# A new order for VectorE, ScalarE and TensorE in the attention stage of a gated cross-attention block with routed experts

## The chip, the cores and the metric

The kernel runs on one core of a Trainium2 chip. The time is the device time of one execution in microseconds (us). The five engines of the core work through their own lists of instructions, each strictly in order, and meet only at semaphores: TensorE (PE: matmuls, transposes), VectorE (DVE), ScalarE (ACT), GpSimd (POOL) and SyncE (SP, which here only starts transfers).

## The reference

Eight sequences of 112 tokens with 512 channels, and for each a context of 375 tokens. The block computes:

```python
x = x + tanh(g_xattn) * xattn(layernorm(x), ctx)
x = x + tanh(g_ffn)   * experts(layernorm(x))

def xattn(h, cond):                      # 16 query heads in 8 groups, head size 128
    ln_out = ln(h)
    q, k, v, qx = fp8_linear(ln_out, ...)     # inputs rounded to fp8, times weights
    kx, vx = split(cond @ w_kv_x)
    q, k, qx, kx = ln(q), ln(k), ln(qx), ln(kx)   # per head, over 128 values
    core = softmax(q k^T / sqrt(d)) v         # 112 x 112 per head
    xout = softmax(qx kx^T / sqrt(d)) vx      # 112 x 375 per head
    return fp8(concat(core, xout) / smooth) @ wproj * scale

def experts(x):                          # 8 experts, the best 2 per token
    return sum_i w_i * (silu(x @ Wg[i]) * (x @ Wu[i])) @ Wd[i]
```

## The kernel before

There are four stages: quantising the inputs (to about 60 us), attention (to about 845 us), the output projection (to about 980 us), and the experts. The change is in attention alone.

Attention runs over four groups of heads (four query heads each, `g`), and within a group over the eight sequences. A position `(g, u)` is one step. Queries and keys are made in tiles of 128 rows (seven tiles for 896 tokens), so that the positions u = 0 to 6 have a tile and u = 7 has none. The work is a pipeline of two: step `s` projects position s, while the position before, `t`, goes through softmax and the product with the values. I call the attention part of one t a unit; it is counted from the first score matmul of t to the first of the next.

In an ordinary step PE does: project 0 (queries), transposes of the normed queries of t (turn 0, 1), project 1 (cross queries), turn 2 (keys) and turn 3 (cross keys), project 2, the self scores (`p_self`) and two of four cross scores (`p_cross`), turn 4, project 3, the transposes of the softmax results (turn_self, turn_cross 0), cross score 2, turn_cross 1, cross score 3, project 4, outputs 0 (`p_out`), turn_cross 2 and 3, project 5, outputs 1.

The parts of a step on the other engines:
- ACT: `take` j (L689) empties the PSUM bank of projection j and writes the squares of its values; `turned` n (L713) writes a transposed piece with weight and bias; `exp_self` (L734) and `exp_cross` h (L743); `c_high` (L666), the high part of a context chunk. take 3, 4 and 5 wait until turn 4 of the unit before has read `nkx`.
- POOL: `c_low` k (L615), the low part `c_lo` of a context chunk, 128x500, and `rstd` j (L598), which makes `rs`, the reciprocal root of the variance, for the rows of projection j. It goes through them as c_low 0, rstd 0, c_low 1, rstd 1, c_low 2, rstd 2, rstd 3, rstd 4, rstd 5.
- DVE: `sums` j (L1025) adds up the squares, `scale` j (L1034) multiplies `nq` (j = 0), `nqx` (1), `nk` (2) or a part of `nkx` (3 to 5) by `rs`; `max_self` (L1042), `max_cross` h (L1056), `norm_self` (L1048), `norm_cross` h (L1062); `take_self` (L1069) and `take_cross` h (L1074) copy transposed results out of PSUM (`pselfT`, `pcrossT`); `inputs` (L1016) fills `xqs` for the next step; `smoothed` (L1080) empties `p_out`; `exponents` and `rounded` (L1087, L1098) round the result to fp8 and write `cat`.

The order on each engine is written out by hand in functions `step` and, for positions without a tile, `last_step` (ACT L771, L750; PE L953, L929; DVE L1139, L1106). The steps are named: "first" is the very first, "queries" is u = 6 and "keys" u = 7 of the groups 0 to 2, in which weights of the next group are split as well, "new" is u = 0 of groups 1 to 3. In group 3 and in the very last step, which projects nothing (A is false), there is no weight work. Each engine waits only at its own next instruction: one that isn't ready holds back all behind it.

Of the kernel before, what the change touches and what calls it, by code (L numbers as in the profile page):

```python
# [396 lines left out]
def before(pos):  # L397
    g, u = pos
    return (g, u - 1) if u > 0 else (g - 1, B - 1)
# [42 lines left out]
def attention(nc, c, sb, ps, sem, ctxT, wproj, catd, vec, ident, mhalf, epst, xq, smi,  # L442
# [207 lines left out]
    def _(act):  # L650
# [99 lines left out]
        def last_step(s, t, g, change):  # L750

            turned(t, 0)
            turned(t, 1)
            take(s, 2)
            turned(t, 2)
            c_high(s, 1)
            if change == "keys": w_high(g, 2, change)
            turned(t, 3)
            exp_self(t)
            exp_cross(t, 0)  # L760
            exp_cross(t, 1)
            turned(t, 4)
            take(s, 3)
            c_high(s, 2)
            if change == "keys": w_high(g, 3, change)
            take(s, 4)
            exp_cross(t, 2)
            exp_cross(t, 3)
            take(s, 5)
# [43 lines left out]
    def _(pe):  # L813
# [139 lines left out]
        def step(s, t, g, change, k):  # L953
            A, Q = s is not None, t is not None
# [10 lines left out]
            if not A: score_self(t)  # L965
            if Q: turn(t, 3)
            if A: project(s, 2, g)
            if A and Q: score_self(t)
# [19 lines left out]
    def _(v):  # L988
# [13 lines left out]
        def w_low(g, n):  # L1002

            v.wait_ge(wh_done[n], g + 1)
            split_low(v, n).then_inc(wl_done[n], 1)
# [100 lines left out]
        def last_step(s, t, g, change):  # L1106
# [5 lines left out]
            if change == "keys": rounded(before(t))  # L1112
# [10 lines left out]
            norm_cross(t, 3)  # L1123
            take_cross(t, 2)
            take_cross(t, 3)
            smoothed(t, 0)
            if change == "keys": inputs((s[0] + 1, 0))
            scale(s, 4)
            if change == "keys": w_low_half(g, 1, 1)
            smoothed(t, 1)  # L1130
            scale(s, 5)
            if change == "keys":
                w_low(g, 2)
                w_low(g, 3)
            else:
                exponents(t)
                rounded(t)

        def step(s, t, g, change, k):  # L1139
# [5 lines left out]
            if change == "new": w_low(g, 4)  # L1145
            if Q: max_self(t)
            if Q: max_cross(t, 0)
            if Q: max_cross(t, 1)
            if change == "new": exponents(before(t))
            if Q: norm_self(t)  # L1150
            if Q: norm_cross(t, 0)
            if Q: norm_cross(t, 1)
            if Q: take_self(t)
            if A: sums(s, 1)
            if Q: take_cross(t, 0)
            if Q: max_cross(t, 2)
            if A: scale(s, 0)
            if Q: take_cross(t, 1)
            if Q: max_cross(t, 3)
            if A: sums(s, 2)  # L1160
            if Q: norm_cross(t, 2)
            if Q: norm_cross(t, 3)
            if A: scale(s, 1)
            if A: scale(s, 2)
            if A: inputs((s[0], s[1] + 1))
            if change == "new": rounded(before(t))
# [10 lines left out]
            if Q and change != "queries": rounded(t)  # L1177
# [729 lines left out]
```

## Time and profile before

Three runs took 1220.67, 1217.78 and 1221.2 us, median 1220.67.

| | |
|---|---|
| the profiled execution's own time | 1220.67 us |
| its span, first to last instruction | 1218.2 us |
| busy: PE, DVE, ACT, POOL | 1096.6, 805.3, 726.3, 495.4 us |
| 32 units of attention | from 90.5 to about 843 us |
| PE clock granted, attention stage | 1.0 of full speed from 81 to 845 us |
| DVE `nq` scale, 28 in all | mean 718 ns |
| DVE `ysum` and `cat` (rounded), 32 each | mean 623 and 625 ns |

A busy time is a mean over stages with different limits. PE is busy 99% of most of the attention stage. There the timeline of one unit tells more: an engine's row gives the start, the duration, and in brackets how long the engine had been idle and whose work ended the wait. Instructions of one engine overlap at their ends, so that the distance of two starts is often somewhat shorter than the first one's duration.

### The profile page before, as it was taken

The numbers are of one execution on the slowest core, as the hardware profiler recorded it, in microseconds if no ns is written. First come the engines' busy times: TensorE is split into PE (matmuls) and PEld (weight loads), VectorE is DVE, ScalarE is ACT, GpSimd is POOL, SyncE is SP. The second block draws the span as 40 slices with busy tenths as digits, with TensorE's granted clock in tenths as the row PEclk, the third lists the DMA queues.
The fourth block names the chain that finished last, engine by engine and source line by source line (L and its number), as shares of the span: only waits on it lengthen the run. The fifth ranks groups of instructions, "written<-read, shape, count | busy, mean of one in ns | idle before, by whom it ended". The sixth has DMA issues, their size and how long they took to land. (4 is left out here: it accounts for less than half of the span.)

```text
span 1218.2 us, 19518 instructions
## 1 busy us (share of the span) xinstructions
PE 1096.6 (90%) x5656; PEld 895.5 (74%) x5656; DVE 805.3 (66%) x1611; ACT 726.3 (60%) x2082; POOL 495.4 (41%) x584
## 2 busy tenths in 40 slices
PE   1089999999999999999999999995999839999996
PEld 1068888778888877888877888874888727777885
DVE  7967877897788787777788777676334675564100
ACT  7967878855888865688875655762121514343432
POOL 3064544444545435444535454440000314565432
PEclk9589999999999999999999999998999759999999
DMA  5042111105111115111112311101546255865220
GB/s 199 0 175 65 43 34 41 52 15 198 50 42 43 34 34 200 39 41 51 42 34 80 107 42 34 49 26 46 178 147 233 90 203 177 246 182 163 48 44 0
DMA packets 51713, 107.38 MB, mean 88 GB/s; under 512 B 5984, under 2 KB 26464, under 8 KB 49568
## 3 DMA queue, kind: packets, MB, share of 16 engines
q1 hardware_dynamic: 46912, 97.00, 24.3%
q0 software_dynamic: 4704, 9.18, 3.3%
q8 instruction: 49, 0.80, 0.3%
q14 instruction: 48, 0.39, 0.1%
HBM read 91.48 MB, written 16.52 MB: 89 GB/s over the span
## 5 line engine op out<-in xcount | busy, mean ns | idle before, releaser
L618 POOL TENSOR_TENSOR c_lo<-c_raw,c_hi 128x500 fp32r<-128x500 f32 x96 | 123.9, 1291 | 208.9 <-ACT c_hi L669 208.9
L612 POOL TENSOR_TENSOR rs<-va,mhalf 125x2 f32<-125x2 f32 (+1 forms) x180 | 199.3, 1107 | 14.3
L827 PE MATMUL p_proj<-w_hi,xqs 128*128 128x512 f32 (+2 forms) x464 | 157.4, 359 | 42.3 <-DVE w_lo L540 41.0
L854 PE MATMUL p_proj<-w_hi,c_hi 128*125 128x512 f32 x384 | 164.5, 429 | 1.3 <-POOL c_lo L618 1.3
L854 PE MATMUL p_proj<-w_hi,c_lo 128*125 128x512 f32 x384 | 151.4, 394 | 0.0
L854 PE MATMUL p_proj<-w_lo,c_hi 128*125 128x512 f32 x384 | 151.4, 394 | 0.0
L827 PE MATMUL p_proj<-w_lo,xqs 128*128 128x512 f32 (+2 forms) x464 | 148.2, 340 | 0.0
L827 PEld LDWEIGHTS p_proj<-w_hi,xqs 128*128 128x128 f32 (+1 forms) x464 | 86.7, 187 | 51.0 <-issue 43.0
L605 POOL TENSOR_TENSOR va<-ss,epst 125x2 f32<-125x2 f32 (+1 forms) x180 | 45.9, 255 | 167.6 <-DVE ss L1030 99.0
L747 ACT ACTIVATE pcross<-p_cross,nmax 112x375 f32<-112x375 f32 x128 | 73.6, 584 | 51.3 <-DVE nmax L1059 51.2
L897 PE MATMUL p_cross<-kxT,qxT 128*112 128x375 f32 x256 | 97.7, 484 | 0.8 <-ACT kxT L723 0.8
L1321 PE MATMUL p_acc<-p_hi,p_catr 128*128 128x512 f32 x224 | 89.0, 397 | 9.1 <-DVE p_lo L1366 9.1
L827 PEld LDWEIGHTS p_proj<-w_lo,xqs 128*128 128x128 f32 (+1 forms) x464 | 86.9, 187 | 8.2
L1321 PE MATMUL p_acc<-p_lo,p_catr 128*128 128x512 f32 x224 | 88.7, 396 | 0.0
L854 PEld LDWEIGHTS p_proj<-w_hi,c_hi 128*125 128x125 f32 x384 | 71.4, 186 | 21.2 <-issue 3.3
L854 PEld LDWEIGHTS p_proj<-w_hi,c_lo 128*125 128x125 f32 x384 | 71.2, 186 | 17.8
L854 PEld LDWEIGHTS p_proj<-w_lo,c_hi 128*125 128x125 f32 x384 | 71.4, 186 | 17.1
L924 PE MATMUL p_out<-pcrossT,valx 125*128 125x224 f32 x384 | 83.7, 354 | 0.0
L1291 ACT ACTIVATE p_hi<-shared 128x512 fp32r<-128x512 f32 x32 | 20.2, 634 | 90.3 <-PE p_acc L1321 80.0
L924 PEld LDWEIGHTS p_out<-pcrossT,valx 125*128 125x128 f32 x384 | 73.2, 191 | 0.3
L1082 DVE TENSOR_TENSOR yb<-p_out,smg 128x448 bf16<-128x448 f32 x64 | 39.7, 621 | 50.9 <-PE p_out L924 50.9
L709 ACT ACTIVATE nkx<-p_proj 125x256 f32<-125x256 f32 x96 | 38.4, 400 | 58.2 <-PE p_proj L854 58.2
(240 smaller groups left out, 2852.5 us busy)
## 6 DMA issues: line engine op xcount, KB each, us to landing
c_raw<-in_ctxT SPq DMA_DIRECT2D x96, 250.0 KB, 2.6
shared<-in_w_in SPq DMA_DIRECT2D x16, 1024.0 KB, 9.0
shared<-in_wproj SPq DMA_DIRECT2D x32, 256.0 KB, 2.9
raw_g<-in_Wg SPq DMA_DIRECT2D x8, 1024.0 KB, 6.6
raw_u<-in_Wu SPq DMA_DIRECT2D x8, 1024.0 KB, 6.9
raw_d<-in_Wd SPq DMA_DIRECT2D x8, 1024.0 KB, 5.7
cat_scratch<-cat SPq DMA_DIRECT2D x32, 224.0 KB, 2.0
shared<-cat_scratch SPq DMA_DIRECT2D x2, 1792.0 KB, 8.2
```

The lines of the kernel that those rows point to most:

```text
L605: pool.tensor_tensor(va[0:rows, lo:hi], ss[0:rows, lo:hi], epst[0:rows, lo:hi], ALU.add).then_inc(va_done, 1)
L612: pool.tensor_tensor(rs[0:rows, lo:hi], va[0:rows, lo:hi], mhalf[0:rows, lo:hi], ALU.pow).then_inc(rs_done, 1)
L618: pool.tensor_tensor(flat(c_lo[:, k, :, :]), flat(c_raw[:, k, :, :]), flat(c_hi[:, k, :, :]).bitcast(F32), ALU.subtract).then_inc(cl_done, 1)
L709: act.activation(nkx[0:CT, j - 3, :], bank[0:CT, 0:256], ACT.Copy)
L747: act.activation(pcross[0:T, h, :], p_cross[0:T, h % 2, 0:TC], ACT.Exp, bias=nmax[0:T, 4 + h:5 + h], accum_out=lsum[0:T, 4 + h:5 + h]).the ...
L827: m = pe.matmul(out, xqs[:, n, k, 0:rows], (w_hi, w_lo)[i % 2][:, k, lo:lo + w], start=(i == 0), stop=(i == 2 * KB - 1))
L854: m = pe.matmul(bank[0:CT, :], a[:, ch, k, :], w[:, k, CKX:CV], start=(i == 0), stop=(i == 3 * KB - 1))
L897: pe.matmul(p_cross[0:T, h % 2, 0:TC], qxT[:, t[1] % 2, h, :], kxT[:, h // HPG, :], start=True, stop=True).then_inc(sx_rdy, 1)
L924: m = pe.matmul(p_out[:, HPG * T:2 * HPG * T], valx[0:CT, par, k, g * P:(g + 1) * P], flat(pcrossT[0:CT, k, HPG * g:HPG * (g + 1), :]), st ...
L1082: v.tensor_tensor(yb[:, g * 4 * T:(g + 1) * 4 * T].rearrange("p (a t) -> p a t", t=T), p_out[:, 0:4 * T].rearrange("p (a t) -> p a t", t=T ...
L1291: act.activation(w_hi[:, n % 2, :], w_raw[:, n % 4, :], ACT.Copy).then_inc(hi_done, 1)
L1321: m = pe.matmul(acc[:, j, :], catr[:, n % 2, j * P:(j + 1) * P], w[:, n % 2, :], start=(first and part == 0), stop=(last and part == 1), s ...
```

## The change

Three engines get another order in attention; no instruction's work is altered. On ACT, take 3 moves ahead of exp_self in the steps without a tile. On PE the self scores move behind turn 3 in the very last step. On DVE, `sums` 1 moves ahead of `max_self` and `scale` 0 ahead of `max_cross` 0 in all steps that project a tile, and `sums` 2, `scale` 1 and `scale` 2 each move up a place; `exponents` and `rounded` of the unit before move up in a "new" step; `rounded` moves from the "keys" step into the end of the "queries" step; and in steps without a tile `inputs`, `scale` 4 and one piece of `w_low` move up.

```diff
@@ ACT, last_step
             turned(t, 3)
+            take(s, 3)
             exp_self(t)
             exp_cross(t, 0)
             exp_cross(t, 1)
             turned(t, 4)
-            take(s, 3)
             c_high(s, 2)
@@ PE, step
             if Qt: turn(t, 2)
-            if not A: score_self(t)
             if Q: turn(t, 3)
             if A: project(s, 2, g)
-            if A and Q: score_self(t)
+            if Q: score_self(t)
@@ DVE, last_step
             max_cross(t, 1)
-            if change == "keys": rounded(before(t))
             norm_self(t)
...
             norm_cross(t, 3)
+            if change == "keys": inputs((s[0] + 1, 0))
+            scale(s, 4)
             take_cross(t, 2)
             take_cross(t, 3)
             smoothed(t, 0)
-            if change == "keys": inputs((s[0] + 1, 0))
-            scale(s, 4)
             if change == "keys": w_low_half(g, 1, 1)
+            if change == "keys": w_low(g, 2)
             smoothed(t, 1)
             scale(s, 5)
             if change == "keys":
-                w_low(g, 2)
                 w_low(g, 3)
@@ DVE, step
             if change == "new": w_low(g, 4)
+            if A: sums(s, 1)
+            if change == "new": exponents(before(t))
             if Q: max_self(t)
+            if A: scale(s, 0)
             if Q: max_cross(t, 0)
             if Q: max_cross(t, 1)
-            if change == "new": exponents(before(t))
             if Q: norm_self(t)
             if Q: norm_cross(t, 0)
             if Q: norm_cross(t, 1)
+            if change == "new": rounded(before(t))
             if Q: take_self(t)
-            if A: sums(s, 1)
+            if A: sums(s, 2)
             if Q: take_cross(t, 0)
             if Q: max_cross(t, 2)
-            if A: scale(s, 0)
+            if A: scale(s, 1)
             if Q: take_cross(t, 1)
             if Q: max_cross(t, 3)
-            if A: sums(s, 2)
+            if A: scale(s, 2)
             if Q: norm_cross(t, 2)
             if Q: norm_cross(t, 3)
-            if A: scale(s, 1)
-            if A: scale(s, 2)
             if A: inputs((s[0], s[1] + 1))
-            if change == "new": rounded(before(t))
...
-            if Q and change != "queries": rounded(t)
+            if Q: rounded(t)
```

In an ordinary step, DVE's list before, from the first sums to the second. `ss<-sq` is sums, `nmax` the maxima, `linv` the reciprocals, `pselfT` take_self; the scale of `nq` comes three rows further down:

```order
L1030 TENSOR_REDUCE ss<-sq 128x4
L1045 TENSOR_REDUCE nmax<-p_self 112x4
L1059 TENSOR_REDUCE nmax<-p_cross 112x1 x2
L1051 RECIPROCAL linv<-lsum 112x4
L1053 TENSOR_TENSOR pself<-pself,linv 112x448
L1064 RECIPROCAL linv<-lsum 112x1
L1066 TENSOR_SCALAR pcross<-pcross,linv 112x375
L1064 RECIPROCAL linv<-lsum 112x1
L1066 TENSOR_SCALAR pcross<-pcross,linv 112x375
L1072 COPY pselfT<-p_tr 112x448
L1030 TENSOR_REDUCE ss<-sq 128x4
```

The same place after (line numbers are one less):

```order
L1029 TENSOR_REDUCE ss<-sq 128x4 x2
L1044 TENSOR_REDUCE nmax<-p_self 112x4
L1038 TENSOR_TENSOR nq<-nq,rs 128x512
L1058 TENSOR_REDUCE nmax<-p_cross 112x1 x2
L1050 RECIPROCAL linv<-lsum 112x4
L1052 TENSOR_TENSOR pself<-pself,linv 112x448
L1063 RECIPROCAL linv<-lsum 112x1
L1065 TENSOR_SCALAR pcross<-pcross,linv 112x375
L1063 RECIPROCAL linv<-lsum 112x1
L1065 TENSOR_SCALAR pcross<-pcross,linv 112x375
L1071 COPY pselfT<-p_tr 112x448
L1029 TENSOR_REDUCE ss<-sq 128x2
```

The second sums and the scale of `nq` have moved from behind take_self to the two sides of max_self.

ACT in a "keys" step, before (-) and after (+). `kxT` is turned 3 and then turned 4, `nkx`, `valx` and `sqx` are take 3, `pself` and `pcross` the exponentials:

```order
 L723 ACTIVATE kxT<-p_cross,vec 128x375
-L739 ACTIVATE pself,lsum<-p_self,nmax 112x112 x4
-L747 ACTIVATE pcross,lsum<-p_cross,nmax 112x375 x2
-L723 ACTIVATE kxT<-p_tr,vec 128x375
-L709 ACTIVATE nkx<-p_proj 125x256
-L710 ACTIVATE valx<-p_proj 125x256
-L685 ACTIVATE sqx,ss<-p_proj 125x128 x2
+L709 ACTIVATE nkx<-p_proj 125x256
+L710 ACTIVATE valx<-p_proj 125x256
+L685 ACTIVATE sqx,ss<-p_proj 125x128 x2
+L739 ACTIVATE pself,lsum<-p_self,nmax 112x112 x4
+L747 ACTIVATE pcross,lsum<-p_cross,nmax 112x375 x2
```

The four reads of take 3 have moved ahead of the four exponentials of the self scores, the two of the cross scores and turned 4.

## Rows read from the trace of the kernel before

**Rows 1.** List of waits, PE: engine, line, released by: us in total, times, longest.
```profile
PE p_out L921 <- DVE pcrossT L1077: 8.6, 24, 1.4
```
**Rows 2.** Timeline, PE, an ordinary unit: start us, us, engine, line, instruction [idle before].
```profile
331.27 0.94 PE L890 MATMUL p_self<-kT,qT 128*112 128x112 f32 x8
...
336.43 0.55 PE L904 MATMUL p_tr<-ident,pself 112*112 112x112 f32 x4
...
337.79 0.55 PE L911 MATMUL p_tr<-ident,pcross 112*125 112x112 f32 x3
...
346.05 0.39 PE L854 MATMUL p_proj<-w_lo,c_hi 128*125 128x512 f32 x1
346.27 0.39 PE L854 MATMUL p_proj<-w_hi,c_lo 128*125 128x512 f32 x1
346.87 0.65 PE L921 MATMUL p_out<-pselfT,val 112*128 112x224 f32 x2 [0.21 <-DVE pcrossT L1077]
...
355.54 0.94 PE L890 MATMUL p_self<-kT,qT 128*112 128x112 f32 x8
```
**Rows 3.** Timeline, DVE, the same unit.
```profile
332.25 0.62 DVE L1045 TENSOR_REDUCE nmax<-p_self 112x4 f32<-112x448 f32 x1 [1.58 <-PE p_self L890]
...
334.39 0.18 DVE L1051 RECIPROCAL linv<-lsum 112x4 f32<-112x4 f32 x1 [0.33 <-ACT pself L739]
334.60 0.63 DVE L1053 TENSOR_TENSOR pself<-pself,linv 112x448 f32<-112x448 f32 x1
...
335.86 0.42 DVE L1066 TENSOR_SCALAR pcross<-pcross,linv 112x375 f32<-112x375 f32 x1
337.02 0.62 DVE L1072 COPY pselfT<-p_tr 112x448 f32<-112x448 f32 x1 [0.74 <-PE p_tr L904]
337.56 0.67 DVE L1030 TENSOR_REDUCE ss<-sq 128x4 f32<-128x512 f32 x1
...
339.02 0.68 DVE L1039 TENSOR_TENSOR nq<-nq,rs 128x512 f32<-128x512 f32 x1
```
**Rows 4.** Timeline, ACT, the same unit.
```profile
331.71 0.66 ACT L677 ACTIVATE sq<-p_proj 128x512 f32<-128x512 f32 x1
...
332.91 0.35 ACT L739 ACTIVATE pself<-p_self,nmax 112x112 f32<-112x112 f32 x1
...
334.24 0.58 ACT L747 ACTIVATE pcross<-p_cross,nmax 112x375 f32<-112x375 f32 x1
...
335.33 0.69 ACT L723 ACTIVATE kxT<-p_tr,vec 128x375 f32<-128x375 f32 x1
```
**Rows 5.** Timeline, POOL, the same unit.
```profile
332.41 1.01 POOL L612 TENSOR_TENSOR rs<-va,mhalf 128x4 f32<-128x4 f32 x1
...
333.39 1.26 POOL L618 TENSOR_TENSOR c_lo<-c_raw,c_hi 128x500 fp32r<-128x500 f32 x1
```
**Rows 6.** Timeline, POOL and DVE, the first step of attention.
```profile
75.84 1.27 POOL L618 TENSOR_TENSOR c_lo<-c_raw,c_hi 128x500 fp32r<-128x500 f32 x1
75.91 1.74 DVE L1039 TENSOR_TENSOR nq<-nq,rs 128x512 f32<-128x512 f32 x1 [1.29 <-POOL rs L612]
```
**Rows 7.** Timeline, several engines, a "keys" unit (from 426.1) and a "new" unit (448.5).
```profile
428.34 0.48 PE L881 MATMUL p_tr<-ident,nkx 125*128 125x125 f32 x3
...
431.32 0.41 ACT L709 ACTIVATE nkx<-p_proj 125x256 f32<-125x256 f32 x1
...
432.35 0.68 ACT L669 ACTIVATE c_hi<-c_raw 128x500 fp32r<-128x500 f32 x1
...
428.23 0.99 DVE L1059 TENSOR_REDUCE nmax<-p_cross 112x1 f32<-112x375 f32 x2
...
454.33 0.59 PE L904 MATMUL p_tr<-ident,pself 112*112 112x112 f32 x4 [0.52 <-DVE pself L1053]
...
464.24 0.62 DVE L1104 TENSOR_TENSOR cat<-ysum,ye 128x896 bf16<-128x896 bf16 x1
...
466.28 0.65 PE L921 MATMUL p_out<-pselfT,val 112*128 112x224 f32 x2 [1.40 <-DVE pcrossT L1077]
```

## The prediction

> **What bounds the kernel now.** I read the list of waits first, then the timeline of one ordinary unit of the attention stage engine by engine, then the two odd units at a change of head group. All edits lie in the attention stage; what follows it starts when it ends, so a microsecond lost or won there is one in the total. In the list of waits the largest term of TensorE (PE) that belongs to the units is one on VectorE (DVE): 24 waits for `pcrossT`, 8.6 us in all [rows 1]. So PE works nearly without a stop and the stage can't gain much: its waits are a few tenths of a microsecond in each of 32 units.
>
> An ordinary unit lasts 24.27 us: from the score matmuls `p_self` at 331.27 to the next ones at 355.54 [rows 2]. I count from 331.27; "at 5.16" means 5.16 us after it. PE's only real wait stands near the unit's end: the last projection matmul starts at 346.27 and `p_out` at 346.87 [rows 2]. That is 0.60 us, where the start before is only 0.22 us away (346.05, and 0.23 to 0.24 elsewhere), so the wait is about 0.36 us. It is for the last copy into `pcrossT` (take_cross 3). The list's 24 cases are 20 ordinary units (five per group) and four others. The gain to be had in ordinary units is at most 20 x 0.36 = 7.2 us.
>
> How much room DVE's other results have is read from the same timeline. The softmax chain is: max_self (ends at 1.60), exp_self on ACT (starts at 1.64), the two max_cross, the reciprocal (at 3.12), norm_self (at 3.33 to 3.96), the second norm_cross (starts at 4.59, ends at 5.01), then take_self at 5.75, right after PE's transposes at 5.16 [rows 2 to 4]. PE's second transpose of `pcross` (turn_cross 1) starts at 6.52, 0.15 us after take_self ends at 6.37: it reuses the PSUM bank that take_self empties. So norm_self has some 1.2 us of room, but the chain norm to take_self to turn_cross 1 has only what take_self waits for: 0.74 us idle before it [rows 3].
>
> **The change in an ordinary unit.** DVE now does sums 1 before max_self, and scale 0 (the tensor_tensor on `nq`) between max_self and max_cross 0. Both stood behind take_self before.
> - sums 1 waits for ACT's squares, which end at 0.44 + 0.66 = 1.10 [rows 4]. It starts at 1.14 and holds DVE 0.59 us, the distance from it to the next instruction after 337.56 [rows 3] (0.67 us by itself, less the overlap of its end). max_self starts at 1.73 instead of 0.98, ends at 2.35, and exp_self starts at 2.39: ACT's exp chain is 0.75 us later.
> - scale 0 needs `rs`, which POOL finishes at 2.15, and POOL then starts the second c_lo at 2.12 without a gap; it runs 1.26 us, to 3.38 [rows 5]. Here is the point on which the sum rests. Both instructions read two SBUF tensors. In the first step of the stage the same pair met: c_lo started at 75.84 and took 1.27 us, the scale of `nq` started 0.07 us behind it and took 1.74 us [rows 6], where it takes 0.68 us elsewhere [rows 3]. It ended 0.54 us after c_lo. So scale 0, which can only start at 2.26 behind max_self, ends at 3.38 + 0.54 = 3.92, not at 2.94.
> - max_cross 0 and 1 follow at 3.84 to 4.83 (0.99 us for both where PE's scores are there, as at 428.23 [rows 7]), the reciprocal at 4.74, norm_self at 4.95. Between norm_self and take_self the order and the durations stay: the second norm_cross starts 1.26 us after norm_self, ends at 6.63, and take_self runs from 6.55 to 7.17. PE's turn_cross 1 starts 0.15 us later, at 7.32 instead of 6.52: **0.80 us lost**. The other two paths agree or are shorter: norm_self ends at 5.58 and PE's transposes of `pself` go from 5.16 to 5.64, 0.48 late; exp_cross 0 starts at 4.42 instead of 2.97 (max_cross 0 is now last), so turned 4 ends 1.46 later, at 6.21 instead of 4.75 (4.06 and 0.69 long [rows 4]), and turn_cross 0 goes to about 6.27, 0.72 late.
> - Behind that, DVE is shorter by what was moved ahead: sums and scale of `nqx` are moved up, and the wait for the third `rs` mostly goes. I find take_cross 3 ending at about 14.6, while PE, 0.80 late, wants it at 15.24 + 0.80 = 16.0. So the wait of **0.36 us goes**.
>
> The unit becomes 24.27 + 0.80 - 0.36 = 24.71 us. Twenty units: +8.8 us. The last unit with a full tile in each group (four) has no such wait to give back: 4 x 0.80 = +3.2 us.
>
> The Trainium skill, page "SBUF — State Buffer", section "Who interferes with whom", says that a DVE instruction with two SBUF inputs contends with a GpSimd one that reads SBUF, that the first to issue has the shared port pair for its whole length, and that the other blocks fully. The trace's 1.74 us is that, with 0.54 us left after c_lo instead of the full 0.68. By the rule to the letter scale 0 would end 0.14 us later and 24 units would cost 3.4 us more, 1241 in all. I go by the row.
>
> **The unit before and after a change of group (three times).** On ACT take 3 now stands ahead of exp_self. It must wait for PE's transposes turn 4, which read the `nkx` it overwrites: they start at 428.34 and end at 428.82, and exp_self could start at 428.34 before. take 3 is four reads of PSUM, from 431.32 to 432.35, 1.03 us [rows 7]. exp_self so starts at about 429.9 instead of 428.34. DVE there was late for its reciprocal anyway, because of `rounded`, which has gone to the unit before. I get PE about 0.7 us late at that unit's end. In the next unit ("new") DVE does sums 1, three exponents and scale 0 ahead of norm_self, with the exponents now even ahead of max_self, and `rounded`, two instructions of 0.62 us [rows 7], between norm_cross 1 and take_self, on the path that PE waits for. PE waited there already (454.33, the wait before it 0.52 by the row, 0.68 by starts) and again for take_cross 3, 1.40 us by the row [rows 7]. The work that was moved ahead is taken from behind, so the second wait goes while the first grows to about 3.5 us. Net for both units together I take +1.2 us; the bounds are -1.5 (both waits of the row go) and +3. Three times: +3.6 us.
>
> **The last group and the last step.** Here the same move on ACT has less cover: exp_self goes from 1.65 after its `p_self` to about 3.8, 2.2 us later, of which the room of 0.74 and the earlier transposes take a part: +1.2 us. score_self behind turn 3 in the last step is one swap of two short PE groups: +0.1 us.
>
> **Edits at nothing.** inputs and scale 4 ahead of take_cross 2 in the "keys" step: PE there waits for smoothed 0 and its own transposes, and inputs fills this; it is in the 0.7 above. `w_low` of piece 2 before smoothed 1: hidden behind PE's outputs 1. POOL's and SyncE's own orders don't change; c_lo 2 comes later by ACT's delay, and PE needs it only at 12.4 (project 5), so it is covered.
>
> **Sum.** 8.8 + 3.2 + 3.6 + 1.3 = 16.9 us. The profiled execution took 1220.67 us (span 1218.2), which is also the median of the three runs, so 1237.6 us.
>
> **Rivals.** A change of 0.3% (3.7 us) is about what a measurement here can tell from none.
> - *Faster: scale 0 and c_lo don't hold each other.* If scale 0 ended by 2.94, the max_cross would end at 3.85, norm_self would start at 4.08 and end at 4.70, and PE's transposes at 5.16 would find it ready; take_self would come at 5.75 as now. Then 20 x 0.36 = 7.2 us are won, the group changes are about even without the stalls, and 1.3 us is lost in the last group: 1214.8 us. It decides at scale 0's end: up to some 3.1 the chain has room. For it speaks that rows 6 are one of only two such meetings of this form; against it that both were equal, and that POOL's c_lo has no idle before it [rows 5], so DVE can't come first. 8 in 100.
> - *Smaller loss: the delays overlap with waits that I count as room used up.* With half the 0.80, ordinary units are even, the others cost 4 x 0.4, and with 3.6 and 1.3 the sum is +6.5: 1227 us. 10 in 100.
> - *No change:* that, and the group changes gain instead of losing (by 1.5 each, the bound above): 1221. 4 in 100.
> - *Larger loss: the wait for take_cross 3 stays.* scale 2 now stands ahead of the last two norm_cross, and scale 1 can meet the third c_lo; if these give DVE back its delay, 7.2 us are not won: 1244.8 us. 13 in 100.
>
> The forecast itself, 1231 to 1243, has 65 in 100. The chance of slower is 0.65 + 0.10 + 0.13 = 0.88, of the same 0.04, of faster 0.08. The range for 8 in 10 goes from 1226 to 1246: it takes in the small loss and the large one and leaves out the faster case.
>
> **What would show it.** In the trace after: ordinary units 24.7 us apart; 24 scales of `nq` between max_self and max_cross, about 1.65 us long instead of 0.68; a wait of PE before the transposes of `pself` and of `pcross` in every unit with a full tile, and the 24 waits for `pcrossT` before `p_out` gone; in the "new" units a PE wait of over 2 us before take_self's copy is done. PE's granted clock through the attention stage should stay at its upper level, 2.4 GHz (the page's clock line shows no fall there through PE waits of 1.4 us [rows 7]). Wrong at the root would be scales of `nq` of 0.7 us in that place. Wrong in size would be a unit that is late by the full 1.5 us of max_cross, or one with the wait at `p_out` still there.

## The result and the profile after

The changed kernel takes 1236.85 us (median of 4 runs, 1235.88 to 1242.38), the kernel before 1220.93 us beside it (4 runs, 1217.78 to 1222.62). The ratio is 1.0158, 95% interval 1.0138 to 1.0179: 15.9 us slower, where the prediction said 16.9. The profiled execution of after took 1238.48 us with a span of 1236.6 us, 18.4 us more than before. Over all 21 executions of after on record (1235.88 to 1242.56) the median is 1240.6 us, 19.7 us over before; where the text below compares with 1236.85 or with 15.9, it takes the median of the four.

The list of waits of after, PE (us in total, times, longest):

```profile
PE p_tr L904 <- DVE pself L1052: 17.2, 32, 2.2
PE p_out L921 <- DVE yb L1081: 3.8, 4, 1.0
PE p_tr L911 <- ACT kxT L723: 2.3, 8, 0.3
PE p_tr L911 <- DVE pselfT L1071: 1.5, 2, 0.8
```

The 24 waits for `pcrossT` [rows 1] are gone, and PE now waits for norm_self in all 32 units (before in 4). The scales of `nq` in after (ns shortest/median/longest, first and last start):

```profile
L1038 DVE TENSOR_TENSOR nq<-nq,rs x28: 675/1658/1732, 75.9 to 810.0; 128x512 f32<-128x512 f32 x28
```

An ordinary unit after, from 339.71 (answering to the unit from 331.27 before). DVE [rows 3]:

```profile
340.86 0.69 DVE L1029 TENSOR_REDUCE ss<-sq 128x4 f32<-128x512 f32 x1 [1.74 <-ACT sq L677]
341.46 0.61 DVE L1044 TENSOR_REDUCE nmax<-p_self 112x4 f32<-112x448 f32 x1
341.99 1.65 DVE L1038 TENSOR_TENSOR nq<-nq,rs 128x512 f32<-128x512 f32 x1
343.56 0.99 DVE L1058 TENSOR_REDUCE nmax<-p_cross 112x1 f32<-112x375 f32 x2
...
344.68 0.62 DVE L1052 TENSOR_TENSOR pself<-pself,linv 112x448 f32<-112x448 f32 x1
...
346.26 0.61 DVE L1071 COPY pselfT<-p_tr 112x448 f32<-112x448 f32 x1
...
347.99 1.13 DVE L1038 TENSOR_TENSOR nqx<-nqx,rs 128x512 f32<-128x512 f32 x1
```

POOL [rows 5]:

```profile
340.86 1.01 POOL L612 TENSOR_TENSOR rs<-va,mhalf 128x4 f32<-128x4 f32 x1
341.84 1.25 POOL L618 TENSOR_TENSOR c_lo<-c_raw,c_hi 128x500 fp32r<-128x500 f32 x1
```

PE [rows 2]:

```profile
339.71 0.95 PE L890 MATMUL p_self<-kT,qT 128*112 128x112 f32 x8
...
345.36 0.60 PE L904 MATMUL p_tr<-ident,pself 112*112 112x112 f32 x4 [0.32 <-DVE pself L1052]
...
347.08 0.50 PE L911 MATMUL p_tr<-ident,pcross 112*125 112x112 f32 x3
...
355.75 0.54 PE L921 MATMUL p_out<-pselfT,val 112*128 112x224 f32 x2
...
364.31 0.94 PE L890 MATMUL p_self<-kT,qT 128*112 128x112 f32 x8
```

The scale of `nq` starts 0.15 us behind c_lo, takes 1.65 us instead of 0.68 and ends at 343.64, 0.55 us after c_lo (343.09). The maxima, norm_self, norm_cross and take_self follow it without a wait. Of the 28 scales of `nq` 24 take 1.65 to 1.67 us, the one of the first step 1.73 us as before, and the three of the "new" steps 0.68 us. The scale of `nqx` meets the third c_lo and takes 1.13 us instead of 0.68 in the same 24 units. PE's second transposes of `pcross` start 7.37 us into the unit instead of 6.52, and `p_out` no longer waits. The unit lasts 24.60 us.

Where the 18.4 us of span are, by the starts of the first `p_self` of each unit (us, before and after):

| | units | before, each | after, each | difference in all |
|---|---|---|---|---|
| ordinary | 20 | 24.28 | 24.60 | +6.6 |
| started in the "queries" step | 4 | 22.02 | 22.80 | +3.1 |
| "keys" | 3 | 22.40 | 23.18 | +2.3 |
| "new" | 3 | 26.46 | 29.77, 27.77, 28.41 | +6.6 |
| last group's unit without a tile | 1 | 15.82 | 18.61 | +2.8 |
| last unit, to the projection's first `p_acc` | 1 | 23.59 | 20.69 | -2.9 |
| before the first unit | | 90.46 | 91.75 | +1.3 |
| behind attention | | 368.2 | 366.8 | -1.4 |

No edit acts in the stretches of the last two rows. Over the 13 profiled kernels of this case these stretches take 90.5 to 91.9 and 366.8 to 369.7 us, so the total of one profile says no more than within some 3 us. The two rows above them belong together: in the last step `p_self`, with which a unit begins, now stands behind turn 3, and 1.6 us pass from the last unit to the one without a tile by the counting alone.

The "new" units are the surprise. The second of them after, PE:

```profile
466.31 0.59 PE L904 MATMUL p_tr<-ident,pself 112*112 112x112 f32 x4 [1.51 <-DVE pself L1052]
467.19 0.75 PE L911 MATMUL p_tr<-ident,pcross 112*125 112x112 f32 x3 [0.29 <-ACT kxT L723]
467.73 1.46 PE L897 MATMUL p_cross<-kxT,qxT 128*112 128x375 f32 x2
```

POOL and DVE in the same unit:

```profile
457.24 1.26 POOL L618 TENSOR_TENSOR c_lo<-c_raw,c_hi 128x500 fp32r<-128x500 f32 x1 [6.02 <-ACT c_hi L669]
457.30 3.36 DVE L540 TENSOR_TENSOR w_lo<-shared,w_hi 128x2048 fp32r<-128x2048 f32 x1
...
462.01 1.35 DVE L1095 TENSOR_SCALAR ye<-ye 128x896 bf16<-128x896 bf16 x1
463.28 0.61 DVE L1044 TENSOR_REDUCE nmax<-p_self 112x4 f32<-112x448 f32 x1
...
465.62 0.63 DVE L1052 TENSOR_TENSOR pself<-pself,linv 112x448 f32<-112x448 f32 x1
...
467.87 0.62 DVE L1103 TENSOR_TENSOR cat<-ysum,ye 128x896 bf16<-128x896 bf16 x1
468.41 0.62 DVE L1071 COPY pselfT<-p_tr 112x448 f32<-112x448 f32 x1
```

Windows of after, PE (stretch, its length, PE busy and instructions, granted clock, DMA share, GB/s), in the first, second and third "new" unit and behind the second:

```profile
270.00:278.00 8.00, 7.53 (x23) 0.61 0.39 126
466.00:471.00 5.00, 4.41 (x15) 0.66 0.34 88
471.00:476.00 5.00, 5.00 (x28) 1.00 0.33 115
664.00:669.00 5.00, 4.20 (x14) 0.66 0.57 187
```

PE waits 1.51 us for norm_self, where it waited 0.52 [rows 7], then 0.29 us, and in the first and the third of these units another 0.68 and 0.80 us ahead of turn_cross 1. Right behind the waits its clock is at the lower level, 1.2 GHz, for a part of the windows: two cross scores take 1.46 us there, where the same two take 0.80 at the upper level. DVE starts max_self 3.81 us into the unit instead of 1.41, since sums 1, the exponents and a longer `w_lo` stand ahead of it. `w_lo` of this form takes 2.28 us where it meets no c_lo, 2.76 in this place before and 3.36 here. `ye` takes 1.35 us beside a c_lo; elsewhere it takes 0.39 or 0.40. Before, the granted clock was 1.0 from 81 to 835 us; the table ahead of the prediction says to 845, which is wrong:

```profile
835.10:838.40 3.30, 3.30 (x11) 0.50 0.00 0
```

That fall comes up again where the prediction is gone through.

### The profile page after: what moved, and what is told of

Read it like the earlier page. It is cut to its first block and busy times, and to the rows that moved or that the text cites. A ratio compares the mean times of both kernels' runs of the same rounds, so it can differ in the third digit from the quotient of the medians.

```text
span 1236.6 us, 19518 instructions
## 1 busy us (share of the span) xinstructions
PE 1104.4 (89%) x5656; PEld 898.8 (73%) x5656; DVE 817.1 (66%) x1611; ACT 726.4 (59%) x2082; POOL 471.6 (38%) x584
## 5 line engine op out<-in xcount | busy, mean ns | idle before, releaser
L618 POOL TENSOR_TENSOR c_lo<-c_raw,c_hi 128x500 fp32r<-128x500 f32 x96 | 121.3, 1263 | 265.9 <-ACT c_hi L669 264.6
L612 POOL TENSOR_TENSOR rs<-va,mhalf 125x2 f32<-125x2 f32 (+1 forms) x180 | 152.4, 847 | 14.2 <-POOL va L605 0.2
L605 POOL TENSOR_TENSOR va<-ss,epst 125x2 f32<-125x2 f32 (+1 forms) x180 | 68.8, 382 | 155.2 <-ACT sqx L685 155.1
L1029 DVE TENSOR_REDUCE ss<-sq 128x4 f32<-128x512 f32 (+1 forms) x84 | 49.6, 592 | 64.9 <-ACT sq L677 64.9
L854 PEld LDWEIGHTS p_proj<-w_hi,c_hi 128*125 128x125 f32 x384 | 72.5, 189 | 19.7 <-issue 2.3
L911 PEld LDWEIGHTS p_tr<-ident,pcross 112*125 112x125 f32 x384 | 53.5, 191 | 26.5 <-issue 13.7
```

The source lines that it names most:

```text
L605: pool.tensor_tensor(va[0:rows, lo:hi], ss[0:rows, lo:hi], epst[0:rows, lo:hi], ALU.add).then_inc(va_done, 1)
L612: pool.tensor_tensor(rs[0:rows, lo:hi], va[0:rows, lo:hi], mhalf[0:rows, lo:hi], ALU.pow).then_inc(rs_done, 1)
L618: pool.tensor_tensor(flat(c_lo[:, k, :, :]), flat(c_raw[:, k, :, :]), flat(c_hi[:, k, :, :]).bitcast(F32), ALU.subtract).then_inc(cl_done, 1)
L854: m = pe.matmul(bank[0:CT, :], a[:, ch, k, :], w[:, k, CKX:CV], start=(i == 0), stop=(i == 3 * KB - 1))
L911: m = pe.transpose(p_tr[0:CT, 1 - h % 2, k * T:(k + 1) * T], pcross[0:T, h, k * CT:(k + 1) * CT], ident[0:T, 0:T])
L1029: v.tensor_reduce(ss[0:rows, lo:hi], sq[0:rows, j % 2, 0:(hi - lo) * HD].rearrange("p (h d) -> p h d", d=HD), AX, ALU.add).then_inc(rd_don ...
```

## The experiments

All on one core, each timed against the kernel before on the same chip. "Unit" is as above. The medians are of 4 to 10 executions (after: the four). The unit columns are from one profiled execution (us, each; * marks a unit in a part of which the granted clock was at the lower level):

| run | median us | ratio to before, 95% | ordinary | queries | keys | "new" |
|---|---|---|---|---|---|---|
| before | 1220.9 | | 24.28 | 22.02 | 22.40 | 26.47, 26.46, 26.46 |
| after | 1236.9 | 1.0138 to 1.0179 | 24.60 | 22.80 | 23.18 | 29.77*, 27.77*, 28.41* |
| a | 1221.1 | 0.9990 to 1.0036 | 23.91 | 22.10 | 23.18 | 26.97, 28.47*, 26.97 |
| b | 1217.0 | 0.9955 to 0.9984 | 23.91 | 22.08 | 23.19 | 27.71*, 26.04, 26.09 |
| c | 1217.5 | 0.9960 to 0.9987 | 24.28 | 22.03 | 22.41 | 25.53, 25.52, 25.51 |
| d | 1233.3 | 1.0079 to 1.0116 | 24.63 | 22.80 | 22.41 | 27.79*, 26.95, 26.96 |
| e | 1233.8 | 1.0082 to 1.0126 | 24.62 | 22.80 | 23.17 | 27.58*, 25.92, 25.94 |
| f | 1240.7 | 1.0145 to 1.0196 | 24.63 | 22.80 | 23.91 | 26.97, 27.99*, 28.03* |
| g | 1207.1 | 0.9862 to 0.9909 | 23.84 | 22.04 | 22.42 | 25.33, 25.32, 25.33 |
| h | 1213.5 | 0.9924 to 0.9966 | 23.83 | 22.03 | 23.89, 23.89, 25.02* | 25.09, 25.09, 25.09 |
| i | 1241.6 | 1.0135 to 1.0178 | 24.61 | 22.81 | 23.17 | 27.79*, 29.92*, 27.87* |
| j | 1235.2 | 1.0100 to 1.0137 | 24.62 | 22.80 | 22.60 | 28.45*, 26.97, 28.53* |
| k | 1206.3 | 0.9856 to 0.9890 | 23.82 | 22.01 | 22.40 | 25.27, 25.27, 25.29 |

**a. Scale 0 back behind take_self, all else changed.**

```diff
             if Q: max_self(t)
-            if A: scale(s, 0)
             if Q: max_cross(t, 0)
@@
             if Q: take_self(t)
+            if A: scale(s, 0)
             if A: sums(s, 2)
```

> The changed kernel with one edit undone in part: scale 0 (nq) stands behind take_self again, sums 1 stays ahead of max_self. Theory 1 (scale 0 meets POOL's second c_lo and is held by it, 1.65 us instead of 0.68 ahead of the max_cross): without the meeting the ordinary unit goes from 24.60 us to about 23.95, the queries unit loses its 0.8, so about 1221 us. Theory 2 (the later exponentials, because sums 1 stands ahead of max_self, are the cost): nearly nothing changes, 1234 to 1237 us.

1221.08 us. Moving this one instruction brings the ordinary unit from 24.60 to 23.91 and takes back 15.8 of the 15.9 us (19.5 of the 19.7 by all executions of after). The scales of `nq` have a median of 681 ns again. sums 1 still stands ahead of max_self here, so sums 1 ahead costs at most the 0.07 us by which the unit is over g's below.

**b. The changed kernel, the second c_lo on 4 of its 500 columns** in all steps with a tile but the first (that low part of the context is left out).

```diff
+            n = 4 if k == 1 and has_tile(s) and s is not FIRST else KB * CT
-            pool.tensor_tensor(flat(c_lo[:, k, :, :]), flat(c_raw[:, k, :, :]), ...
+            pool.tensor_tensor(flat(c_lo[:, k, :, :])[:, 0:n], flat(c_raw[:, k, :, :])[:, 0:n], ...
```

> The changed kernel, order untouched, but POOL's second c_lo of each step with a tile works on 4 columns instead of 500 (the low part of that chunk is left out, so its results are less exact). Theory 1: scale 0 takes 0.68 us, ordinary unit about 23.9 us, total about 1219.5 us. Theory 2: still about 1237 us, since the order on VectorE is the same.

1217.0 us. DVE's list is that of the changed kernel, word for word, and the loss is gone. DVE in an ordinary unit of b:

```profile
333.12 0.61 DVE L1045 TENSOR_REDUCE nmax<-p_self 112x4 f32<-112x448 f32 x1
333.65 0.68 DVE L1039 TENSOR_TENSOR nq<-nq,rs 128x512 f32<-128x512 f32 x1
```

POOL beside it:

```profile
333.51 0.20 POOL L619 TENSOR_TENSOR c_lo<-c_raw,c_hi 128x4 fp32r<-128x4 f32 x1
```

Same place, same neighbours, a short c_lo: 0.68 us. So the cost is the meeting, not the place. The "new" unit is 0.9 us shorter as well (26.04 and 26.09), since `ye` meets nothing there.

**c. The same on the kernel before**, as the control (the same low part left out).

> The kernel before with the same short second c_lo (the same part left out), as the control for the other: both theories say no change, 1221 us within 2, unit 24.27 us, since nothing on VectorE meets that c_lo in the old order.

1217.5 us, 3.2 less than before and more than I expected. All of it is in the "new" units, 26.46 to 25.52 (2.8 us in three). In an ordinary unit of before the second c_lo meets the maxima and the start of norm_self and costs nothing (24.28 both). In the "new" unit it meets the exponents. DVE before, then c:

```profile
451.75 1.35 DVE L1093 TENSOR_SCALAR ye<-yb 128x896 uint16<-128x896 uint16 x1
```

```profile
451.62 0.40 DVE L1094 TENSOR_SCALAR ye<-yb 128x896 uint16<-128x896 uint16 x1
```

The kernel before had such collisions already, and I had not seen them. Besides these three, norm_cross 2 (`pcross`) takes 1.01 or 1.02 us instead of 0.42 in 27 units, each time beside the third c_lo. DVE and POOL in the ordinary unit of rows 2 and 3:

```profile
341.01 1.01 DVE L1066 TENSOR_SCALAR pcross<-pcross,linv 112x375 f32<-112x375 f32 x1
```

```profile
340.54 1.26 POOL L618 TENSOR_TENSOR c_lo<-c_raw,c_hi 128x500 fp32r<-128x500 f32 x1
```

c leaves these 27 as they are; what they cost comes up again under g. Against this control b is the same within the measurement: beside the collision all of the change comes to nothing (0.37 us won in each ordinary unit, and about as much lost at the changes of group and in the last group).

**d. The kernel before with scale 0 alone moved.**

```diff
             if Q: max_self(t)
+            if A: scale(s, 0)
             if Q: max_cross(t, 0)
@@
             if Q: max_cross(t, 2)
-            if A: scale(s, 0)
```

> The kernel before with one edit of the change alone: scale 0 between max_self and max_cross 0, sums 1 stays where it was. Theory 1: scale 0 waits for rs until 2.19 after p_self, meets c_lo and ends at the same 3.92, so the ordinary unit is 24.6 us as in the changed kernel, the queries unit 0.8 longer, total about 1230 us. Theory 2: exp_self keeps its time, so no loss, 1214 to 1221 us.

1233.34 us: one instruction makes 12.6 of the 15.9 us. DVE and, below, PE in an ordinary unit of d, whose `p_self` starts at 335.85:

```profile
336.83 0.62 DVE L1045 TENSOR_REDUCE nmax<-p_self 112x4 f32<-112x448 f32 x1 [1.58 <-PE p_self L890]
338.04 1.74 DVE L1039 TENSOR_TENSOR nq<-nq,rs 128x512 f32<-128x512 f32 x1 [0.59 <-POOL rs L612]
```

```profile
341.50 0.59 PE L904 MATMUL p_tr<-ident,pself 112*112 112x112 f32 x4 [0.33 <-DVE pself L1053]
```

max_self is on time here, 0.77 us earlier in the unit than in after, and it doesn't matter: scale 0 waits for `rs` and then ends 0.54 us after c_lo (337.98 + 1.26) all the same. c_lo's end sets the unit's chain, so the unit is 24.63 us with and without sums 1 ahead. My 0.59 us for sums 1 was right as a duration and is hidden under c_lo.

**e. The changed kernel, exponents and rounded of the "new" step back in their old places.**

```diff
-            if change == "new": exponents(before(t))
             if Q: max_self(t)
@@
             if Q: max_cross(t, 1)
+            if change == "new": exponents(before(t))
             if Q: norm_self(t)
@@
-            if change == "new": rounded(before(t))
             if Q: take_self(t)
@@
             if A: inputs((s[0], s[1] + 1))
+            if change == "new": rounded(before(t))
```

> The changed kernel with one part undone: in the three "new" steps DVE does the exponents behind max_cross 1 again (they stand ahead of max_self in the changed kernel) and rounded behind inputs again (it stands between norm_cross 1 and take_self). Everything else is as changed. Theory 1, that these moved instructions lie on PE's path to the transposes of pself and pcross and that the long wait there also costs PE its clock: the new unit, 29.8, 27.8 and 28.4 us in the changed kernel, comes down to about 27.3 (26.46 before, plus the 0.8 of scale 0), the stretches of some 3.4 us at the half clock at about 467 and 666 us go, and the keys unit stays at 23.2; total 1236.8 - 4 = about 1233. Theory 2, that the long new unit is the effect of scale 0 and sums 1 alone: the new units stay at 28 to 30 us and the total at 1237.

1233.84 us, as theory 1 said; the falls at 467 and 666 us are gone, one at 270 us stays. (This is 3.0 us under the median of four of after and 6.8 under that of all 21.) The "new" units without a clock fall are 25.93 us (I said 27.3). With the moves such a unit is 26.97 (a, f and j), so they cost 1.04 us a time. PE's waits show where: in f's first "new" unit, with the moves, three, and in e's second, with the moves undone, one.

```profile
268.20 0.59 PE L904 MATMUL p_tr<-ident,pself 112*112 112x112 f32 x4 [1.51 <-DVE pself L1052]
269.09 0.55 PE L911 MATMUL p_tr<-ident,pcross 112*125 112x112 f32 x3 [0.29 <-ACT kxT L723]
...
271.07 0.55 PE L911 MATMUL p_tr<-ident,pcross 112*125 112x112 f32 x3 [0.80 <-DVE pselfT L1071]
```

```profile
464.50 0.59 PE L904 MATMUL p_tr<-ident,pself 112*112 112x112 f32 x4 [1.66 <-DVE pself L1052]
```

The first wait doesn't depend on where the exponents stand (ahead of max_self or behind the maxima, DVE has done them before norm_self). By the waits, what costs is rounded between norm_cross 1 and take_self (0.80 us) and exp_self behind a late max_self (0.29). Neither of these two units had a clock fall; e had one in three "new" units, after three in three.

**f, i, j. The "keys" unit: ACT's take 3 back, DVE's rounded back, both back.**

```diff
@@ f and j: ACT, last_step
             turned(t, 3)
-            take(s, 3)
             exp_self(t)
@@
             turned(t, 4)
+            take(s, 3)
@@ i and j: DVE, last_step and step
             max_cross(t, 1)
+            if change == "keys": rounded(before(t))
             norm_self(t)
@@
-            if Q: rounded(t)
+            if Q and change != "queries": rounded(t)
```

> The changed kernel with ACT's one move undone: take 3 stands behind turned 4 again in the steps without a tile (three keys steps, and the one of the last group). Theory 1, that this move is the loss of 0.78 us in the keys unit: the keys unit goes from 23.18 back to about 22.4 us, three times, and the last group's from 18.61 to about 15.8; but its following unit, 21.25 now, goes up to about 24.2, since the two together lost nothing. Total 1236.8 - 2.3 = about 1234.5. Theory 2, that the keys unit's 0.78 comes from DVE's order (inputs and scale 4 ahead of take_cross 2): it stays at 23.2 and the total at 1237.

> The changed kernel with DVE's one move at the keys step undone: rounded stands between max_cross 1 and norm_self of the keys step again and not at the end of the queries step; ACT's take 3 stays ahead of exp_self. What is open is which edit costs the keys unit its 0.78 us (22.40 before, 23.18 after; with take 3 moved back it was 23.94, with a wait of 0.76 us for c_lo). Theory 1, that two edits each make exp_self late, rounded by making max_self 1.3 us late on DVE and take 3 by holding ACT, and that the later one decides: with only rounded put back take 3 still holds exp_self at 3.9 us, so the keys unit stays at 23.1 to 23.4 and the total at 1237. Theory 2, that rounded alone is the cause: keys unit 22.4, total 1234.5.

> The changed kernel with both undone, rounded back in the keys step and take 3 behind turned 4; inputs, scale 4 and w_low of piece 2 stay moved up in the steps without a tile. Theory 1, that both edits together are the loss and those that stay cost nothing there: the keys unit is 22.4 us as before, three times, the last group's unit near 15.8, total about 1234. Theory 2, that inputs and scale 4 ahead of take_cross 2 cost PE time too (its wait for yb at p_out was 0.81 us before and 0.99 after): keys unit 22.6 or more.

f failed its expectation: undoing take 3 made the unit longer, 23.91. In the queries step rounded now stands ahead of max_self, so max_self starts 2.94 us into the unit (1.62 before). exp_self is then late by itself, and with it turned 4, take 3 and c_high 2 behind it on ACT. PE, in f and then in j:

```profile
444.08 0.47 PE L854 MATMUL p_proj<-w_hi,c_hi 128*125 128x512 f32 x1 [0.76 <-POOL c_lo L618]
```

```profile
441.66 0.47 PE L854 MATMUL p_proj<-w_hi,c_hi 128*125 128x512 f32 x1 [0.44 <-POOL c_lo L618]
```

With rounded put back and take 3 ahead (i) the unit is 23.17, as in after: now ACT's four reads hold exp_self. With both back (j) it is 22.60. So either edit alone makes exp_self late: it starts 3.59 us into the unit in f, 3.89 in i and in after, 2.27 in j and before. With rounded moved, take 3 ahead even saves 0.73 us, since c_lo then comes in time. The last 0.20 us over before is what remains moved in j, `inputs` and scale 4 ahead of take_cross 2: PE's wait for `yb` at `p_out` is 0.98 us there and 0.81 before. The medians of f and i are 3.8 and 4.7 us over after's median of four, but 0.05 and 1.0 us over that of all 21, so neither differs from after by more than executions do among themselves.

**g. The kernel before, with two instructions in DVE's idle times:** sums 1 behind max_cross 1, scale 0 behind norm_cross 1.

```diff
             if Q: max_cross(t, 1)
+            if A: sums(s, 1)
@@
             if Q: norm_cross(t, 1)
+            if A: scale(s, 0)
             if Q: take_self(t)
-            if A: sums(s, 1)
@@
             if Q: max_cross(t, 2)
-            if A: scale(s, 0)
```

> The kernel before with only this: sums 1 directly behind max_cross 1 (the idle time of 0.33 us before the reciprocal), scale 0 directly behind norm_cross 1 (the idle 0.74 us before take_self), so that neither stands ahead of a maximum and scale 0 starts after the second c_lo has ended. Theory 1, that ordinary units can win only the wait for pcrossT at p_out and that this place costs nothing: scale of nq 0.68 us, ordinary units 23.8 to 23.95 us instead of 24.27, twenty times, new and keys units as before; total 1220.7 - 7 = about 1214. Theory 2, that anything ahead of take_self delays PE's transposes of pcross: units 24.2 to 24.4 us and 1221 or a little more.

1207.07 us, 1.15% faster than before. It reaches what the change was after, DVE's later work done earlier, without meeting c_lo: `nq` takes 682 ns (median), and there is no wait at `p_out`, PE in an ordinary unit of g, 10.32 us and 15.29 us into it:

```profile
337.71 0.54 PE L921 MATMUL p_out<-pselfT,val 112*128 112x224 f32 x2
...
342.68 0.54 PE L921 MATMUL p_out<-pselfT,val 112*128 112x224 f32 x2
```

The gain is 0.44 us in each of 20 ordinary units (8.7 us) and 1.14 in each "new" unit (3.4 us). I had expected 7 in all. The wait in rows 2 was read as 0.36 us and is worth 0.44; in the "new" units the wait of 1.40 us for take_cross 3 [rows 7] is gone, and one of 0.54 us ahead of turn_cross 1 has come. The order is not the whole reason. With sums 1 early POOL does the third c_lo 6.17 us into the unit instead of 9.27, it no longer meets norm_cross 2, and all 128 scalings of `pcross` take 0.41 or 0.42 us. Those 0.6 us a unit are more than the wait of 0.44, so the second collision alone could account for it; no run separates the two.

**h. g, with the exponents of the "new" step behind take_self and one `w_low` of the "keys" step behind max_cross 2**, into 1.72 us of DVE idle time.

```diff
-            if change == "new": exponents(before(t))
@@
             if Q: take_self(t)
+            if change == "new": exponents(before(t))
@@ last_step
             max_cross(t, 2)
+            if change == "keys": w_low(g, 2)
             scale(s, 3)
```

> The kernel of the run with sums 1 behind max_cross 1 and scale 0 behind norm_cross 1, and at the change of group: exponents of the new step behind take_self instead of behind max_cross 1, and w_low of piece 2 in the keys step behind max_cross 2 instead of behind smoothed 1. Theory 1, that PE's 0.5 and 1.4 us waits in the new unit are for DVE work that has room elsewhere: the new unit goes from 26.46 to about 25 us, three times; total about 1210. Theory 2, that the exponents only change places with another wait (for take_cross 3): the new unit stays within 0.5 us of 26.46 and the total is that of the other run, about 1214.

1213.47 us, slower than g by 6.4 us, which neither theory had. DVE, POOL and PE of h:

```profile
428.82 0.54 DVE L1059 TENSOR_REDUCE nmax<-p_cross 112x1 f32<-112x375 f32 x1
429.27 1.21 DVE L540 TENSOR_TENSOR w_lo<-shared,w_hi 128x1024 fp32r<-128x1024 f32 x1
```

```profile
428.86 2.73 POOL L618 TENSOR_TENSOR c_lo<-c_raw,c_hi 128x500 fp32r<-128x500 f32 x1 [6.71 <-ACT c_hi L669]
```

```profile
431.73 0.47 PE L854 MATMUL p_proj<-w_hi,c_hi 128*125 128x512 f32 x1 [1.91 <-POOL c_lo L618]
```

In DVE's idle time POOL was at work on c_lo: now DVE runs at its usual speed (1.21 us), c_lo takes 2.73 us instead of 1.25, and PE waits for it. In the third group the clock fell behind this wait as well (that "keys" unit is 25.02 us, the others 23.89).

**k. g with the exponents alone moved.**

> The kernel of the run with sums 1 behind max_cross 1 and scale 0 behind norm_cross 1 (1207.1 us) with only the exponents of the new step moved behind take_self; w_low of piece 2 in the keys step stays behind smoothed 1. In the run that had both of these moves the keys unit was 23.89 instead of 22.43, c_lo took 2.73 us beside w_low and PE waited 1.91 us for it, and the new unit was 25.09 instead of 25.33. Theory 1, that w_low beside c_lo is the whole loss of that run: keys unit 22.4, c_lo 1.25 us there, new unit 25.1, total 1207.1 - 0.7 = about 1206.4. Theory 2, that the loss came from elsewhere: keys unit over 23 and the total near 1213.

1206.27 us, ratio to before 0.9873 (0.9856 to 0.9890). c_lo is back at 1.25 us and the "keys" unit at 22.40: `w_low` beside c_lo was the loss of h. The exponents' place is worth 0.05 us a unit (25.28 for 25.33, I said 25.1), so k and g are equal within the measurement; the rest of h's shorter "new" unit, 25.09, came with `w_low`'s move. Both beat both kernels.

## Why the prediction was right, point by point

- **The collision, the root of it: right, and shown.** Said: scale 0 takes 1.65 us between max_self and max_cross and ends 0.54 us after c_lo. Measured: 1.65 us, 0.55 us after c_lo. b removes the collision and keeps the place, a removes the place; both remove the loss. The rival without a collision was put at 1214.8 us; b, less what c alone brings, makes it about 1220, no change: that rival's ordinary units were right (0.37 won), and its group changes weren't even.
- **Ordinary unit, said +0.80 - 0.36, measured +0.33.** The first term is 0.69 to 0.76: with scale 0 ahead the unit is 24.60 us, with it behind take_self 23.91 (a), in g 23.84. The chain came as said, PE's transposes of `pself` 5.65 us into the unit (said 5.64) and turn_cross 1 at 7.37 (said 7.32); a wait of its own before the transposes of `pcross`, also said, stands in no row of this unit. The second term was too small: the wait is worth 24.28 - 23.84 = 0.44 us and not 0.36. Together twenty units cost 6.6 us and not 8.8. The reading that this wait is take_cross 3's own place in DVE's list missed the stretched norm_cross 2 ahead of it (c).
- **Queries unit, said +0.80, measured +0.78.** Four times: 3.1 against 3.2.
- **The larger-loss rival, wait for take_cross 3 stays:** fallen, only one wait of 0.9 us is left of those in [rows 1]. Its mechanism does occur, `nqx` meets the third c_lo and takes 1.13 us, but this doesn't reach PE.
- **Change of group, said +3.6 us, measured +8.9.** This is the term that failed. "keys": I said 0.7 us late, it is 0.78, though by a cause that I had only half (rounded in the queries step makes max_self late too, 2.94 us into the unit instead of 1.62). "new": I netted a growing first wait against a vanishing second one and came to 0.5 us a time. Without a clock fall that is the measured number, 26.97 against 26.46, but by luck: a first wait grown from 0.5 to 3.5 us, less the 1.40, makes 1.6 us more than before, and I took 0.5. Measured are 1.51, 0.29 and 0.80 us, 2.6 in all, where before had 0.52 and 1.40; no single wait is over 2 us, as I had named for a sign. What I missed is the clock. I wrote that it should stay at its upper level, since PE's waits of 1.4 us had caused no fall before. The trace of before did show a fall inside attention, from 835.05 us, behind a wait of 2.23 us and one of 0.29 (its rows stand under the next point); I had read the clock line of the page alone. In after it fell in all three "new" units, for 0.8, 1.4 and 2.8 us (27.77, 28.41 and 29.77 less 26.97), 5.0 us in all. Before, PE's waits there were 0.52 and 1.40 us and 12 us apart; in after they are 1.51, 0.29 and up to 0.8 us within 3 us. What in these waits brings a fall no run isolates.
- **Last group, said +1.3, measured -0.1: both terms as said but for 0.1, hidden by a clock fall.** The unit without a tile is 2.79 us longer and the last unit 2.90 shorter. Of both, 1.6 us is the counting (`p_self` behind turn 3): with take 3 back the unit without a tile is 17.43 (f) or 17.42 (j), against 15.82. Take 3 ahead costs the other 1.19 us, where I said 1.2. (f's expectation of 15.8 for that unit missed the counting too.) `p_self`'s move itself costs nothing, where I said 0.1: from the last `p_out` that waits for `yb` to the transposes of `pself` it is 8.17 us before (824.88 to 833.05) and after (845.93 to 854.10). PE before, in its last unit:

```profile
833.05 0.60 PE L904 MATMUL p_tr<-ident,pself 112*112 112x112 f32 x4 [2.23 <-DVE pself L1053]
...
834.33 0.80 PE L897 MATMUL p_cross<-kxT,qxT 128*112 128x375 f32 x2
834.96 0.71 PE L911 MATMUL p_tr<-ident,pcross 112*125 112x112 f32 x3
835.47 1.46 PE L897 MATMUL p_cross<-kxT,qxT 128*112 128x375 f32 x2
```

  Before spent 3.4 us at the lower clock there. After had the same wait of 2.23 us and no fall behind it. Where the changed order has that fall too (e and i), its last unit is 21.98 us instead of 20.69 and the two together are 40.59, against 39.41 before: +1.2 us. The profiled execution of after was spared a fall.
- **"Edits at nothing":** `w_low` before smoothed 1 shows no cost, though no run has it alone; inputs and scale 4 cost 0.2 us in the "keys" unit (j).

In the profile the terms add up to 18.4 us of span: 16.9, less 2.2 for ordinary units, plus 5.3 for the group changes, less 1.4 for the last group, and 0.2 less for the rest. By the medians beside each other it is 15.9, by all 21 executions of after 19.7. Of the 20 that were not profiled here 14 took longer than the profiled one, and 12 have a mean granted clock of 0.951 to 0.953 over the execution, where it has 0.955. So most had more time at the lower clock, not less, and by all executions the forecast is 3 us short, where by the four it is 0.8 too long. That it is this near is in part luck: errors of both signs met, ordinary units 2.2 too dear and the clock falls left out, 5 us in the profile.

## What to carry to other kernels

Before an instruction is moved into an idle time, look at what the other engine that works in SBUF does in that time (here POOL with its c_lo), and not only at who waits for the moved instruction. Here 0.68 us of work placed beside a c_lo cost 0.7 to 0.8 us a unit; placed 2.8 us later, with sums 1 moved as well, the unit gained 0.44. An idle time of DVE beside a busy POOL isn't free (h), and a stall that is already in the kernel shows as one duration of a form that is three times the others (1.35 against 0.40 us) or more than twice (1.01 against 0.42).

## What the runs showed of the hardware

- Two-input instructions of DVE in SBUF and POOL's c_lo hold each other up: 0.68 to 1.65 or 1.74 us for `nq` (after, d), 0.68 to 1.13 for `nqx` (after), 2.28 to 3.36 for `w_lo` (after), 1.25 to 2.73 us for c_lo (h). A tensor_scalar of DVE is hit too, 16-bit (0.40 to 1.35 us for `ye`, before against c) and fp32 (0.42 to 1.01 for `pcross`, before).
- Who loses can't be read from the starts. In after c_lo starts 0.15 us ahead of `nq` and DVE is held; in h c_lo starts 0.41 us ahead of `w_lo` and c_lo is held: it ends at 431.59, 1.11 us after `w_lo`, about its own length. The Trainium skill, page "SBUF — State Buffer", section "Who interferes with whom", says that the one that issues first has the pair and the other blocks for its whole length. The blocking agrees with h (2.73 us); the order of the starts in the trace does not. The idle time ahead of POOL's instruction doesn't sort the cases either: c_lo comes after 6.71 us of it in h and is held, and after 6.02 us of it in after's "new" unit, 0.06 us ahead of `w_lo`, and DVE is held. What decides is open.
- The loser doesn't always pay its whole length behind the winner: `nq` ended 0.54 or 0.55 us after c_lo, where alone it takes 0.68.
- PE's granted clock fell from 2.4 to 1.2 GHz inside attention, in a part of the executions of the same waits. In the "new" units it fell in 11 of 15 with waits of 1.5, 0.29 and up to 0.8 us close together (after, a, f, i, j), in one of three each with a single wait of 1.67 (e) or 1.98 us (d), and in one of three with 0.59, 0.29 and 0.80 us (b); never in the 15 with 0.52 and 1.40 us, 12 us apart, or less (before, c, g, h, k). Behind the 2.23 us in the last unit it fell in all six profiles with the old order there and in four of seven with the new. A fall cost a "new" unit 0.8 to 3.0 us.
